# A decoder layer in one launch: scores and transposes side by side on TensorE, V split on GpSimd, new orders for all engines

## What is computed

```python
q, k, v = (einsum('ntc,hdc->nhtd', layernorm(x), w) for w in (w_q, w_k, w_v))
a = softmax(where(causal, q @ k.T / 8, -inf))          # per sequence and head, 512 x 512
x = x + concat_heads(a @ v) @ w_o
x = x + cross_attention(layernorm(x), ctx, mask, Wq, bq, Wk, bk, Wv, bv)   # 64 context rows
h = silu(n @ w1.T * s1) * (n @ w2.T * s2)              # n = layernorm(x)
x = x + gelu(gelu(h @ h1.T * sh1) @ h2.T * sh2) @ w3.T * s3
```

## Time and profile before

| | us |
|---|---|
| median of 3 runs | 1463.36 (1463.03 to 1465.83) |
| the profiled execution, its own time | 1464.81 |
| its span in the trace | 1463.0 |
| PE busy | 1441.9 (99%) |
| DVE busy | 1240.6 (85%) |
| ACT busy | 1020.1 (70%) |
| POOL busy | 482.2 (33%) |
| mean granted clock of PE | 0.997 |

### The profile page before, as it was taken

One profiled execution on the slowest core, in us unless ns is written; L12 is line 12 of the kernel. 1 busy time (PEld: TensorE's weight loads), 2 busy tenths in 40 slices (PEclk: granted clock), 3 DMA queues, 4 the chain that ended last, 5 costly groups with the idle time before them and its releaser, 6 DMA issues.

```text
span 1463.0 us, 28987 instructions
## 1 busy us (share of the span) xinstructions
PE 1441.9 (99%) x10408; PEld 1228.4 (84%) x10408; DVE 1240.6 (85%) x3068; ACT 1020.1 (70%) x2382; POOL 482.2 (33%) x755
## 2 busy tenths in 40 slices
PE   8999999999999999999998999999999999999998
PEld 6888888888888888888887788888888888888887
DVE  7999999999999999999899957788776748888876
ACT  6888888888888888887788855554456445555644
POOL 2444555454655555555544221202111100000000
PEclk9999999999999999999999999999999999999999
DMA  4000100101001001010012444544342593041310
GB/s 159 2 1 2 59 2 16 45 1 43 18 1 59 2 16 45 2 59 2 16 30 101 163 149 176 194 146 144 130 144 99 199 322 117 30 145 60 115 59 30
DMA packets 78276, 113.53 MB, mean 78 GB/s; under 512 B 4768, under 2 KB 54304, under 8 KB 77216
## 3 DMA queue, kind: packets, MB, share of 16 engines
q1 hardware_dynamic: 78112, 111.32, 22.2%
HBM read 71.45 MB, written 42.99 MB: 78 GB/s over the span
## 4 chain that ended last, share of the span: by engine, by line
PE 88%; DVE 8%; ACT 2%; issue 2%; DMA 1%; SPq 0%; DVEq 0%
PE bank L1457 11%; PE bank L847 11%; PE bank L767 9%; PE bank L819 8%; PE bank L1301 8%; PE bank L769 7%; PE bank L768 7%; PE bank L1303 7%; PE bank L831 6%; PE bank L1475 4%; PE bank L1427 2%; PE bank L1418 2%; PE bank L1416 2%; PE bank L1420 2%; DVE P L1008 1%
## 5 line engine op out<-in xcount | busy, mean ns | idle before, releaser
L1038 POOL TENSOR_SCALAR P<-P,stats 128x128 f32<-128x128 f32 (+3 forms) x512 | 268.1, 541 | 254.5 <-DVE stats L1016 254.5
L903 ACT ACTIVATE P<-P,stats 128x384 f32<-128x384 f32 (+3 forms) x512 | 286.8, 568 | 30.5 <-DVE stats L1008 28.8
L1008 DVE CUSTOM_DVE_ANT_0 P<-bank,cmask 128x384 f32<-128x384 f32 (+3 forms) x512 | 226.0, 482 | 8.0 <-PE bank L819 7.0
L917 DVE TENSOR_TENSOR PT<-bank,PT 128x512 fp32r<-128x512 f32 (+1 forms) x384 | 210.1, 593 | 11.2 <-ACT PT L870 8.7
L1457 PE MATMUL bank<-op,ws 128*128 128x512 f32 x896 | 205.9, 390 | 0.0
L1301 PE MATMUL bank<-Hb,hw 128*128 128x512 f32 x512 | 201.4, 393 | 0.8 <-DVE Hb L1660 0.8
L1457 PEld LDWEIGHTS bank<-op,ws 128*128 128x128 f32 x896 | 167.3, 188 | 34.1
L870 ACT ACTIVATE PT<-bank 128x512 fp32r<-128x512 f32 (+1 forms) x384 | 176.3, 537 | 22.3 <-PE bank L831 20.6
L847 PE MATMUL bank<-PT,V 128*128 128x512 f32 (+3 forms) x1024 | 178.8, 322 | 3.5 <-DVE PT L917 3.5
L847 PEld LDWEIGHTS bank<-PT,V 128*128 128x128 f32 x1024 | 163.1, 190 | 22.0 <-DVE PT L917 4.6
L1303 PE MATMUL bank<-Hb,hw 128*128 128x512 f32 x448 | 174.8, 390 | 0.0
(11 more groups left out here) (246 smaller groups left out, 3141.1 us busy)
## 6 DMA issues: line engine op xcount, KB each, us to landing
h_scratch<-go SPq DMA_DIRECT2D x64, 256.0 KB, 2.1
src<-h_scratch SPq DMA_DIRECT2D x16, 1024.0 KB, 6.8
xs<-x_scratch SPq DMA_DIRECT2D x15, 512.0 KB, 4.1
ws<-ws_scratch SPq DMA_DIRECT2D x7, 1024.0 KB, 7.7
x_scratch<-x SPq DMA_DIRECT2D x8, 512.0 KB, 3.6
x_scratch<-xs SPq DMA_DIRECT2D x8, 512.0 KB, 3.0
xg<-x_scratch SPq DMA_DIRECT2D x8, 512.0 KB, 3.9
out<-xg SPq DMA_DIRECT2D x16, 256.0 KB, 2.1
```

What stands on the lines that cost most here:

```text
L903: e.activation(p, p, ACT.Exp, bias=st_[:, k:k + 1], scale=-1.0, accum_out=st_[:, 8 + k:9 + k]).then_inc(s_exp, 1)
L917: return e.tensor_tensor(dst, a, b.bitcast(f32), ALU.subtract)
L1008: e.tensor_tensor_reduce(P_tile(P, i, a), banks["S", P, max(i, 1)][a][:, slice(*S_COLS[i])], cmask[:, 512 - n:512], -1.0, 3.0e38, ALU.add, ...
L1038: e.tensor_scalar(p, p, stats[P % 4][:, k:k + 1], 1.0, ALU.mult, ALU.mult).then_inc(s_norm, 1)
```

## The change

It has five parts.

1. **One run in a period.** PE's order becomes k, v, q, AV, AV, O, S.P, T.(P-1). The scores of a pair stand directly ahead of the transposes of the pair before. In the steady part there is one run a period instead of two; counted in PE's order, the runs of the attention go from 131 to 69.
2. **Shared banks.** `T.(P-1).2` writes the left half of the two banks whose right half `S.P.1` has just filled, so it makes no claim of its own. Block 0 of the scores moves from the step `S.P.1` to `S.P.2`. A period takes 16 banks. New waits keep PE, DVE and ACT apart in the shared banks: `m.P.1` waits for `T.(P-1).2`, and `ph.(P-1).2` waits for `m.P.1`.
3. **V.** ACT copies the bank to one of two buffers `vtmp` (`vc`), and the bank is free then. POOL makes the high and the low part from the copy (`vh`, `vl`). DVE makes none.
4. **Y** has three buffers instead of four, to make room for `vtmp`.
5. **Orders.** `HEAD`, `BATCH` and `TAIL` give way to one table `ATTENTION`, all its orders new on all engines; its start has `k.0 q.0 v.0` ahead of `S.0`, where `v.0 k.0 q.0 k.1 v.1 v.2` stood. In `pair`, `go.p.0` comes after the first quarter of product 4 instead of ahead of it, and in the last pair `Gl.3.2.m` comes ahead of the addition `c12.3.(m-1)` on DVE.

Of the tables one line each:

```diff
-HEAD = {
+ATTENTION = {
     "PE": """
-        idle.0 rows.0.0 rows.0.1 idle.1 v.0 k.0 q.0 k.1 v.1 v.2 S.0.3 S.0.2 S.0.1 q.1 v.3 S.1.3 S.1.2 k.2
+        idle.0 idle.1 rows.0.0 rows.0.1 k.0 q.0 v.0 S.0.3 S.0.2 S.0.1 k.1 q.1 v.1 v.2 S.1.3 v.3 S.1.2 S.1.1
...
-BATCH = {
...
@@ pair
             o.append(("prod", p, i, m))
+            if (i, m) == (4, 0):
+                o.append(("go", p, 0))
             if new[0] < B // 2:
                 o += [("oh", *new, m), ("ol", *new, m)]
+            if last and i == 6:
+                o += split(p, 2, m)
...
-            if i in (5, 6):
+            if i == 5 or i == 6 and not last:
                 o += split(p, i - 4, m)
...
-        if i in (3, 5):
-            o.append(("go", p, i // 4))
+        if i == 5:
+            o.append(("go", p, 1))
@@ buffers
-    Yb = [at(L + 164 + 4 * i, f"Y{i}", [128, 2, 512], f32r) for i in range(4)]
+    Yb = [at(L + 164 + 4 * i, f"Y{i}", [128, 2, 512], f32r) for i in range(3)]
+    vtmp = [at(L + 176 + 2 * i, f"vtmp{i}", [128, 512]) for i in range(2)]
...
-    S_COLS = {3: (0, 512), 2: (0, 384), 1: (0, 256), 0: (256, 384)}
+    S_COLS = {3: (0, 512), 2: (0, 384), 1: (256, 512), 0: (384, 512)}
+    S_ITEM, S_TILES = {3: 3, 2: 2, 1: 1, 0: 2}, {3: (3,), 2: (2, 0), 1: (1,)}
@@ dealing out banks
+        elif item[0] == "T" and item[2] == 2 and last == ("S", item[1] + 1, 1):
+            shared.add(item[1])
+            banks[item], earlier[item] = banks[last], []
...
         if kind == "v":
-            return s_vlo, n + 1
+            return s_vall, n + 1
@@ ACT
-        def v_high(n):
-            Hf, t = divmod(n, 4)
+        def v_copy(n):
             w.wait_ge(s_v, n + 1)
-            w.wait_ge(s_av, 8 * (Hf - 1))
...
+            if n > 1:
+                w.wait_ge(s_vlo, n - 1)
+            copy(vtmp[n % 2][:, :], bank["v", n][:, :]).then_inc(s_vall, 1)
...
         def pt_high(P, u, h):
             w.wait_ge(s_T, T_at[P, u])
+            if u == 2 and P in shared:
+                w.wait_ge(s_max, max_at[P + 1, 1, h])
@@ DVE
-        def v_low(n):
...
             w.wait_ge(s_S, at_S(P, i))
+            if i == 1 and P - 1 in shared:
+                w.wait_ge(s_T, T_at[P - 1, 2])
@@ POOL
+        def v_high(n):
+            w.wait_ge(s_vall, n + 1)
+            w.wait_ge(s_av, 8 * (n // 4 - 1))
+            e.tensor_scalar(v_part(n, 0), vtmp[n % 2][:, :].rearrange("p (q a d) -> p q a d", q=4, a=2), 1.0, 1.0, ALU.mult,
+                            ALU.mult).then_inc(s_vhi, 1)
+
+        def v_low(n):
+            w.wait_ge(s_vhi, n + 1)
+            e.tensor_tensor(v_part(n, 1), vtmp[n % 2][:, :].rearrange("p (q a d) -> p q a d", q=4, a=2),
+                            v_part(n, 0).bitcast(f32), ALU.subtract).then_inc(s_vlo, 1)
...
         def y_high(P):
             w.wait_ge(s_y, 2 * P + 2)
-            if P >= 4:
-                w.wait_ge(s_o, 2 * ((P - 4) // 2) + 2)
+            if P >= 3:
+                w.wait_ge(s_o, 2 * ((P - 3) // 2) + 2)
```

More of the change, by code:

```diff
@@ new lines @@
+        idle.0 idle.1 rows.0.0 rows.0.1 k.0 q.0 v.0 S.0.3 S.0.2 S.0.1 k.1 q.1 v.1 v.2 S.1.3 v.3 S.1.2 S.1.1
+        T.0.2 T.0.0 T.0.1 k.2 q.2 AV.0.0 AV.0.1 v.4 S.2.3 S.2.2 S.2.1 T.1.2 T.1.0 k.3 q.3 T.1.1 v.5 AV.1.0
+        AV.1.1 S.3.3 S.3.2 T.2.0 S.3.1 T.2.2 T.2.1 k.4 q.4 v.6 AV.2.0 AV.2.1 O.1 S.4.3 S.4.2 S.4.1 T.3.2 T.3.0
+        T.3.1 v.7 k.5 q.5 rows.1.0 rows.1.1 AV.3.0 AV.3.1 O.2 S.5.3 S.5.2 S.5.1 T.4.2 T.4.1 T.4.0 v.8 k.6 q.6
+        AV.4.0 AV.4.1 O.3 S.6.3 S.6.2 S.6.1 T.5.2 T.5.0 T.5.1 v.9 k.7 q.7 AV.5.0 AV.5.1 O.4 S.7.3 S.7.2 T.6.0
@@ L278, in steps @@
     return [(k, *map(int, a)) for k, *a in (t.split(".") for t in text.split())]
-def batch(engine, c):
-    out = []
-    for t in BATCH[engine].split():
-        kind, lag, *a = t.split(":")
-        if kind in ("ls", "lc", "rs", "ln0", "ln2", "tt2", "rows", "rows_high", "rows_low"):
-            n, end = c + int(lag), B
-        else:
-            n, end = 8 * c + 6 + int(lag), NP + (kind in ("O", "os"))
-        if n < end:
-            out.append((kind, n, *map(int, a)))
-    return out
 BY_BLOCK = 2
@@ L467, in pair @@
     return o
-LOOP = range(1, 5)
-ORDER = {engine: steps(HEAD[engine]) + [i for c in LOOP for i in batch(engine, c)] + steps(TAIL[engine])
-         for engine in BATCH}
+ORDER = {engine: steps(ATTENTION[engine]) for engine in ATTENTION}
 for _engine in ORDER:
@@ L641, in program @@
     STAGED = {(0, 0): 2, (0, 1): 3, (1, 0): 8, (1, 1): 5}
-    banks, earlier = {}, {}
-    user, turn = [None] * 8, 0
+    banks, earlier, shared = {}, {}, set()
+    user, turn, last = [()] * 8, 0, None
     for item in ORDER["PE"]:
@@ L652, in program @@
             use = (4, 5) if item[2] == 0 else (6, 7)
+        elif item[0] == "T" and item[2] == 2 and last == ("S", item[1] + 1, 1):
+            shared.add(item[1])
+            banks[item], earlier[item] = banks[last], []
+            for j, k in enumerate(use):
+                user[k] += ((item, j),)
+            last = item
+            continue
         elif item[0] in ("S", "T"):
@@ L659, in program @@
         banks[item] = [psum[k] for k in use]
-        earlier[item] = [user[k] for k in use if user[k] is not None]
+        earlier[item] = [u for k in use for u in user[k]]
         for j, k in enumerate(use):
-            user[k] = (item, j)
+            user[k] = ((item, j),)
+        last = item
     bank = {item: b[0] for item, b in banks.items()}
@@ L669, in read_done @@
         if kind == "S":
-            return s_max, max(max_at[n, i, j] for i in ((1, 0) if a[1] == 1 else (a[1],)))
+            return s_max, max(max_at[n, i, j] for i in S_TILES[a[1]])
         if kind == "T":
@@ L814, in scores @@
             w.wait_ge(s_qklo, 2 * P + 2)
-            for i in ((1, 0) if i0 == 1 else (i0,)):
+            for i in S_TILES[i0]:
                 qs, at = slice(i * 128, i * 128 + 128), slice(*S_COLS[i])
```

609 lines of the change are left out of this document (359 added, 250 removed).

## The result

| | before | after |
|---|---|---|
| median of the runs, us | 1463.26 (1463.03 to 1465.83) | 1445.32 (1444.80 to 1445.53) |
| the profiled execution, its own time, us | 1464.81 | 1444.80 |
| its span, us | 1463.0 | 1443.0 |

The ratio is 0.987, with a 95% interval of 0.9858 to 0.9882: faster by 17.9 us, 1.3%. Run again later beside before on one chip it was 1445.06 against 1463.70. The forecast was 1441.0, the range 1435 to 1457.

What follows compares the result with a forecast made beforehand. In the steady attention PE waits for nothing, so only less PE work shortens it. 19.8 (runs) + 2 (start) + 1.5 (`go.p.0`) - 1 (layer norm) = 22.3 us, from 1463.36 to 1441.0 us; range 1435 to 1457.

Steps and rivals of the forecast that it cites:

- runs: Attention on PE: 131 runs become 69, each costing 0.32 us at its edges, so 19.8 us gained.
- start: Start of the program: PE's waits for rows of x and banks of v shrink; 0 to 4 us gained, 2 taken.
- layer norm, batch boundaries: Periods where DVE makes a block's four statistics: 1.5 us extra work leaves no margin; 1 us lost for six blocks.
- end of the attention: New order round PE's wait of 2.93 us, still only short fillers ahead: no change, 3 us either way.
- last stage: `go.p.0` waits covered by a quarter of product 4, the last pair's end unchanged: 1.5 us gained, between 0 and 2.
- `go.p.0`: Its 0.5 us waits for the last `Gl` are covered by a quarter of product 4: 1.5 us gained.
- The cover: Steady attention: DVE, ACT and POOL loads and chains fit a period of 11.61 us, so PE gets no new wait.
- The chain called the thinnest: POOL in steady attention: v, its copy, `vh`, `vl`, eight `n`, then T; half a microsecond to spare.
- rival A: POOL is late: V's parts (`vh` at 992 ns) or hand-overs cost more; 1446 to 1459 us, chance 0.20.
- D: Start and end orders cost 4 us more each, 1449 us; sign: first AV later than 38 us; bad part's chance 0.05.
- B: Steady attention: V's split on POOL becomes the bound and the kernel gets slower, 1490 us; chance 0.07.
- C: The edge's price doesn't go with the runs, S to T costs as much: 1461 us, no change; chance 0.04.

Runs made afterwards that it cites:

- e1: The changed kernel with the first S step ahead of O in periods 12 to 48, one narrow run more in each: 1476.39 us, ratio to before 1.008.
- e3: The changed kernel with the order of the last stage (`pair`) as it was before the change: 1449.26 us.
- e5: The changed kernel with V's low half made twice on POOL for tiles 14 to 53, ahead of the `n` steps: 1463.44 us, beside before at 1463.98.
- e12: The changed kernel with V split on ACT and DVE for tiles 12 to 53, block transposes earlier, and attention-end steps moved on DVE and POOL: 1441.74 us.

## Why the prediction was right, and where it was off

The mechanism was right for the runs, which are nearly all of the gain, and the time lies 4.3 us above the forecast. The sum by its terms, all from the two profiled executions:

| term | forecast | measured | how |
|---|---|---|---|
| runs | 19.8 | 19.2 to 19.8 | 62 x 0.31 to 0.32; e1's 0.34 would make it 21.1 |
| start | +2 | +2.2 | see below |
| layer norm, batch boundaries | -1 | -2.6 | 1.5 the transfer of batch 6, 0.7 `ln0.7` and `ln2.7` beside V on POOL, 0.4 in batch 7 |
| end of the attention | 0 | -0.7 | not measured by itself: what is left up to the first gate, with 19.8 for the runs |
| gates and MLP | 0 | -1.7 | 378.3 us against 376.6 |
| last stage | +1.5 | +3.0 | 269.1 against 272.1; 2.2 `go.p.0`, 0.8 the last pair |
| sum | 22.3 | 20.0 | |

*Runs.* Right, and e1, which adds runs, shows the price rather than only fitting it. Single slots were off by 0.05 each way (S 2.02 for 1.97, T 1.34 for 1.39), the period was 11.64 for 11.61.

*The cover.* DVE's share of the stretch, forecast at 90, is 92.9, hardly less than the 93.2 of before. Over one batch DVE is busy 86.2 us where it was 89.2 (425.21 to 518.27, and 442.59 to 538.11 before), so 3.0 less, though V's low halves were 4.8 of it: the scaling of the layer norm takes 2.3 us a batch beside POOL's work instead of 1.3, and the rest is small differences. The forecast took every other DVE step at its old price. POOL's, 72, is 71.2. `vh` costs 620 ns and `vl` 1300, as taken, so rival A's 992 did not come. The chain called the thinnest is the right one; its margin was 0.9 where 0.5 was worked out. The overlap in the mean duration of `n` (512 x 541 ns against 268.1 us busy) is 0.14 of the difference; the rest was not traced.

*The failed step* is "Layer norm: ... I take 1 us in all for six blocks", which measured 2.6. It looked at DVE's statistics. It did not look at what else a batch boundary puts into a queue, nor at what V's work on POOL does to the DVE step that it stands beside (`ln0.7` and `ln2.7`, 0.7 us). The order tables show the rows a pair earlier on POOL, ahead of `n`, and the prediction, which asked of every moved step what stands behind it, did not ask it of these. They wait for a way through DRAM that begins with DVE's block transposes, and its last landing was anything from 2.8 to 5.1 us in the two executions of the changed kernel. The price, 0.75 and 1.5 us in these two, is small. The term is off by 1.6, as much as the two others that missed: the last stage (1.5), and the gates and MLP (1.7), for which the sum had no term at all.

*`go.p.0`.* Right mechanism, size off: it gave 2.2 us, not 1.5, since each of its three waits cost 0.74 where the earlier trace rows name 0.5. The fourth wait was that of the last pair's end, which the prediction left as it was; the new place of `Gl.3.2.m` removed it, 0.8 us that the sum had at nothing.

*Start.* The size came out, the reason did not. PE's waits there sum to 3.7 us now (1.67, 1.71 and 0.36) and did to 4.1. What differs is the granted clock: 0.83 in the stretch of 10 to 20 us in before, 1.00 after. That is 3.4 us at the half, 1.7 us of PE's time. The store of batch 0 stands at 156.32 and 156.84 in two executions with the order of before, both with that stretch at 0.83. With the new order it stands at 145.8 to 146.6 in the seven executions that have the full clock, at 147.1 and 148.0 in two with 0.83 from 30 to 40 us, and at 149.0 and 149.1 in two (e1, e3) with 0.83 in both of these stretches. So the start gives 2.2 us or takes 0.8, by the execution; the first AV comes at 35.0 us in the changed kernel, and at 38.0 and 38.1 in e1 and e3, the 38 that the prediction had as its sign of D. The level of these stretches differs between executions of the same start, and why stays open.

*End and gates.* PE waits more at the end (5.0 us from 750 to 785, 2.02 + 1.28 + 1.00 of it at 773 to 779, for 4.4 from 765 to 806 with the 2.93 of the earlier trace rows) and runs at 1.2 GHz for longer behind it: 0.86, 0.50 and 0.62 of the clock in the three stretches of 5 us from 770 on, where before had 0.62 and 0.53 in two of 2 us. That is 5.1 us of clock against 1.7. What makes up for most of it was not traced. In the gates, 0.9 of the 1.7 is the wait for `flags` (2.13, before 1.25); the rest was not traced.

*Profile and median.* The forecast took 1.5 off, since before's profiled execution stood 1.5 above the median of three. Later medians of before are 1463.3 to 1464.8, and the changed kernel's profiled execution was the fastest of its four, 0.5 under their median. So the 1.5 was one execution's luck and not a property to carry over; 2.3 of the sum, 1.5 and 0.5 are the 4.3.

The rivals: A came in a mild form, not through V's price but through the transfer and through V's neighbour on DVE. B did not; e5 shows how near it is: one more `vl` and the time is that of before. C is out by e1, D by the table, but for the executions with the half clock at the start.

## What to carry to other kernels

Count the switches between kinds of matmul, price one from slots with different neighbours, and merge runs. But ask which buffers the merged steps claim at once, since without the shared claims the same order was 60 us slower than before. When steps move on an in-order queue, list each moved step that waits for a transfer and what stands behind it: its landing varied from 2.6 to 5.1 us here, and the margin, not the mean, says whether that costs. When work moves to another engine, look also at what it will stand beside: here it made a DVE step of 0.4 us take 1.45. And an engine that is idle a third of the time can still be the one that is late: what matters is what stands ahead of the urgent work.

## What the runs showed that was not expected

GpSimd and VectorE slow each other. A POOL instruction of 128x128 took 0.37 us beside a DVE step with one input in a bank, and 1.58 beside a DVE subtraction with both inputs in SBUF. The slowing goes both ways: in e12 the DVE step `w<-stageB,w` took 1.94 us beside POOL's low half of Y instead of 1.22, and an instruction of `ln2.7` above took 1.45 instead of 0.39:

```profile
773.08 1.94 DVE L1824 TENSOR_TENSOR w<-stageB,w 128x1024 fp32r<-128x1024 f32 x1
```

In the steady attention, where nearly all DVE instructions have an input in a bank, V's strided halves on POOL kept their 620 and 1300 ns. The Trainium skill, "SBUF — State Buffer", Who interferes with whom, says that a DVE instruction with two inputs in SBUF contends with a GpSimd one that reads SBUF, and that one with at most one does not unless it runs in a mode that takes both of DVE's ports, which `tensor_scalar` can do. The two-input half agrees with the traces here (1.58 for 0.37, 1.94 for 1.22). `ln2.7` is a TENSOR_SCALAR with one tensor read from SBUF and was slowed all the same (1.45 for 0.39), so only the exception could cover it; in which mode it ran no trace shows.

The last of four parts, 128 KB each, of one small transfer landed after 2.6 to 5.1 us. In the order of before it never took above 3.6 in 12 batches; with the new order it took 3.9 or more in 20 of 72 batches (twelve executions of it and its variants), 16 of the 20 in batches 6 and 7. What it meets there was not found out. One candidate that no run moves is a transfer of 512 KB (`x<-in_x`, in batch 7 `xs<-x_scratch`) which SP issues 0.5 us behind the last part in every batch: in the changed kernel it took 5.9 and 4.9 us in batches 6 and 7, 3.9 to 4.7 in the four others.
